# Joined attentions of a hybrid block: the full-array work of a group in three blocks instead of two

## The chip, the cores and the metric

One core of a Trainium2 chip runs the whole program in one launch. The metric is the time of the program on the device in microseconds (us). TensorE (PE in the profile) multiplies matrices, VectorE (DVE), ScalarE (ACT) and GpSimd (POOL) work on rows of 128 partitions, and PSUM is the memory of eight banks into which TensorE writes.

## The reference

Eight samples of 512 x 128 float32 pass through eight residual layers: attention A, a mixture of experts, attention B, the same mixture of experts, a linear attention, an adapter with experts, an attention with relative positions, and the adapter again. The change touches only attention A and attention B. Each of them is a causal attention with 16 heads of 8 channels:

```
q, k, v = (layernorm(x) @ Wq), (layernorm(x) @ Wk), (layernorm(x) @ Wv)     # 16 heads of 8
dot     = where(causal, q @ k.T * scale, -inf)                              # 512 x 512 for each head
x       = x + softmax(dot) @ v @ Wo
```

## The kernel before

The kernel handles two samples (a and b) in one turn of a loop and takes four turns. In each turn both samples go through the eight layers. `pe_attn(p, ...)` is TensorE's program for one attention layer of both samples at once ("joined"); it is called twice in a turn (p = 0 and 1), so it runs eight times in all.

**Groups and jobs.** The 32 heads (16 of a, then 16 of b) form 8 groups of 4. A group has 12 row jobs and 12 column jobs. A row job (L1049) computes scores with queries on the partitions, so that VectorE can take the row maximum (L1684, `row_max`); a column job (L1088) computes the same scores again, transposed and with the maximum already subtracted from q, so that ScalarE can take the exponential (L742) into `prob4`, and GpSimd then zeroes the diagonal blocks above the causal line (L531). Both kinds contract over 32 partitions only: each job occupies one of four 32-row strips of TensorE's array, and four jobs can run beside each other. A float32 matmul leaves two records in the profile. Row jobs 0 to 3 of a group have 512 columns, jobs 4 to 7 have 384, jobs 8 to 11 have 256 + 128. Column jobs 0 to 3 have 512 columns, 4 to 7 have 384, and 8 to 11 have 256 + 128 in two matmuls.

**The order on TensorE.** The order is written out by hand. Step k of the loop issues row job k and column job k - 16 (`LEAD` = 16). In the code `at` is the column job's number within its group g, so that k modulo 12 is `at` + 4 modulo 12. This text names a step by k modulo 12. Full-array work comes between steps:

- after step 2 the maxima are transposed (`max_columns`, L1059), the weighted heads of an earlier group are transposed back to rows (`head_rows`, L961), and a projection (L1028, "project") follows; `weigh_group(g, [0, 1])` (L1103), the first half of the product of probabilities and values, follows too. It has 16 records of 512 and 384 columns;
- after step 7 comes `weigh_group(g - 1, [2, 3])` (L1103, 16 records of 256 and 128 columns) and another projection.

Projections and a few single pieces of work stand in the table `BEHIND`, by k: at k = 67 the values of sample b are computed as well (L1035), and at k = 79 and 86 the output of sample a is transposed (L1121) and projected (L1129) in place of a projection.

**Buffers.** Row jobs and all full-array pieces but the weighing rotate over four PSUM banks; the order is the list `PLACES`, which is built from `BEHIND`. An entry waits until the entry four places earlier was read (`wait_place`). Column jobs rotate over three banks: job c waits for the exponential of job c - 3. From column job 81 on (`WIDE`, step k = 97) they have five banks. The weighing accumulates in bank 7; ScalarE copies it out after the group's second half (`group_columns`, L709), and `head_rows` waits for that copy. VectorE subtracts the maxima from q (`shift_q`, L1693) and divides the weighted heads by their sums (`heads_out`, L1655, L1656) after its row maximum 2 of each group. ScalarE moves projections out (L726 for q, L728 for k) at the step at which they stand in `BEHIND`.

**The tail.** Row jobs end with k = 95. After it the steps k = 96 to 111 issue column jobs alone, with the layer norm for the mixture of experts behind column job 90 (`HOOK`, L927), and then its router (L1209).

Of the kernel before, what the change touches and what calls it, by code (L numbers as in the profile page):

```python
# [66 lines left out]
ROWS4 = 3 * G4  # L67
GROUPS = 2 * NG
JOBS = ROWS4 * GROUPS
LEAD = 16  # L70
# [1 line left out]
HOOK = JOBS - 6  # L72


BEHIND = {26: [("norm", 0)], 31: [("project", 8)], 38: [("project", 9)], 43: [("project", 10)],
          50: [("project", 11)], 55: [("project", 12)], 62: [("project", 13)], 67: [("values", 0), ("project", 14)],
          74: [("project", 15)], 79: [("out_columns", 0)], 86: [("out", 0)]}
PLACES = []
for k in range(JOBS):
    PLACES.append(("row", k))  # L80
    if k % ROWS4 == 2 and k > ROWS4:
        PLACES.append(("max", k // ROWS4 - 1))
        if k // ROWS4 >= 3:
            PLACES.append(("heads", k // ROWS4 - 3))
    PLACES += BEHIND.get(k, [])
PLACE = {entry: at for at, entry in enumerate(PLACES)}
# [23 lines left out]
def build(nc, a_x, a_wq, a_wk, a_wv, a_wo, b_wattn, b_wout, m_ws, m_bs, m_wg, m_wu, m_wd,  # L110
# [9 lines left out]
    with ExitStack() as ctx:  # L120
# [53 lines left out]
        values = val_row[:, :, 0:H * BELOW].rearrange("p t (h d) -> p t h d", h=H)  # L174
# [22 lines left out]
        stage, at = part(0, [NSTAGE, P])  # L197
        stage_qk, at = part(at, [2, P])
        stage_gate, at = part(at, [P])
        rel_res, at = part(at, [2 * P])  # L200

        q_st, at = part(0, [H // 2, T], BF16)
        k_st, at = part(at, [H // 2, T], BF16)
        ring_at = at
        res, at = part(ring_at, [2, T])
        k_parts, at = part(at, [3, T], BF16)
        q_parts, at = part(ring_at + 3072, [3, T + 2], BF16)
# [12 lines left out]
        q_masked1, at = part(ring_at + 2 * T + 3 * T // 2, [2, IC, NT * H], BF16)  # L220
# [4 lines left out]
        r_neg_max, at = part(ring_at + RING * COLS, [RING, NT])  # L225
        sc, at = part(at, [H, len(BLOCKS), P])
        r_rden, at = part(at, [2, NT, G4])

        silu, at = part(at4, [2, T])
        hidden, at = part(at, [HSLOTS, T])  # L230
        lg, at = part(at, [NT, E])
        gt, at = part(at, [NT, E, E])
        eq, at = part(at, [NT, E, E])
        rank, at = part(at, [NT, E])
        top, at = part(at, [NT])
        lgd, at = part(at, [NT, E])
        ex, at = part(at, [NT, E])
        mixes, at = part(at, [2, NT, E])
        tot, at = part(at, [NT])

        l_qT, at = part(0, [NC2, T])
        l_kT, at = part(at, [NC2, T])
        l_k, at = part(at, [NT, H * DM])
        l_v, at = part(at, [NT, H * DM])
        l_vk, at = part(at, [NT, H * DM])
        l_wt, at = part(at, [2, 2, NT, P])
        l_st, at = part(at, [2, NT - 1, P])
        l_tmp, at = part(at, [2, NT, P])
        l_sq, at = part(at, [2, T])
        l_sqk, at = part(at, [2, 512])  # L250
        l_beta, at = part(at, [NT, H])
        l_ssum, at = part(at, [2, NT, H])
        l_rec, at = part(at, [2, NT, H])
        l_inv, at = part(at, [2, NT, H])

        pooled, at = part(0, [1])
        pool_rep, at = part(at, [P])
        d_hid, at = part(at, [KD, T])
        d_up, at = part(at, [KD, P])
        d_lg, at = part(at, [E])  # L260
        d_negm, at = part(at, [1])
        d_ex, at = part(at, [E])
        d_z, at = part(at, [1])
        d_gt, at = part(at, [E, E])
        d_eq, at = part(at, [E, E])
        d_rank, at = part(at, [E])
        d_w, at = part(at, [E])
        d_s, at = part(at, [1])
        d_w4, at = part(at, [KD])
        d_wT, at = part(at, [P])  # L270
# [3 lines left out]
        def bank(n):  # L274
            return psum[:, n, :]
# [217 lines left out]
        def column_head(c):  # L493

            return (c + 2) % G4

        def pad_bank(i):

            return (3, 7, 4, 5)[i % 4]
# [10 lines left out]
        def column_bank(c):  # L510

            return 3 + c % 3 if c < WIDE else 1 + (c - WIDE) % 5
# [208 lines left out]
        def act_attn(eng, p, scale):  # L721
            def stack(i, bk):
                eng.wait_ge(p_qk, 2 * GROUPS * p + i + 1)
                G = i // 2 % NG
                if i % 2 == 0:
                    m = eng.activation(q4[:, G, :], bank(bk), ACT.Copy, scale=scale)  # L726
                else:
                    m = eng.activation(k4[:, G, :], bank(bk), ACT.Identity, bias=k_one[:, 0:1])  # L728
                m.then_inc(p_st, 1)

            def out_columns(n, bk):
                eng.wait_ge(a_oT, n + 1)
                eng.activation(xnTs[n % 2][:, :], bank(bk), ACT.Copy).then_inc(a_oTs, 1)

            for i in range(2 * NG):
                stack(i, pad_bank(i))
            for c in range(JOBS):
                g, hh, j = c // ROWS4, column_head(c), c % ROWS4 // G4
                if g >= 2 and c % ROWS4 == 0:
                    eng.wait_ge(s_pv, GROUPS * p + g - 1)  # L740
                eng.wait_ge(s_col, JOBS * p + c + 1)
                eng.activation(prob4[:, g % 2, hh, C_AT[j]:C_AT[j] + C_N[j]], bank(column_bank(c))[:, 0:C_N[j]],  # L742
                               ACT.Exp).then_inc(s_exp, 1)
                if g >= 1 and c % ROWS4 == 5:
                    group_columns(eng, (g - 1) // NG, GROUPS * p + g - 1, 7, s_pv, GROUPS * p + g)
                for what, i in BEHIND.get(c + LEAD, []):
                    if what == "norm":
                        act_norm(eng, attn_call(2 * p + 1), row_bank((what, i)))
                    if what == "project":
                        stack(i, row_bank((what, i)))  # L750
                    if what == "out_columns":
                        out_columns(2 * p, row_bank((what, i)))
                if c == HOOK + 2:
                    act_norm(eng, moe_call(2 * p), 6)
            g = GROUPS - 1
            moe_exp(eng, 2 * p)
            group_columns(eng, 1, GROUPS * p + g, 7, s_pv, GROUPS * (p + 1))
            moe_silu(eng, 2 * p, 0)
            out_columns(2 * p + 1, 6)
# [231 lines left out]
        def pe_attn(eng, p, w):  # L991
# [101 lines left out]
            def weigh_group(g, keys):  # L1093

                last = min(keys[-1], 2)
                eng.wait_ge(s_keep, JOBS * p + ROWS4 * g + G4 * (last + 1))
                eng.wait_ge(a_v, 2 * p + g // NG + 1)
                if g >= 1:
                    eng.wait_ge(a_cols, GROUPS * p + g)
                for s in keys:  # L1100
                    for hh in range(G4):
                        h = G4 * (g % NG) + hh
                        m = eng.matmul(bank(7)[32 * hh:32 * hh + 32, P * s:T],  # L1103
                                       val_row[:, s, BELOW * h:BELOW * h + 32],
                                       prob4[:, g % 2, hh, C_COL[s]:C_COL[s] + T - P * s],
                                       start=(s == 0), stop=(s == NT - 1))
                if keys[-1] == NT - 1:
                    m.then_inc(s_pv, 1)
# [50 lines left out]
            for k in range(3 * NG, JOBS + LEAD):  # L1159
                if k < JOBS:  # L1160
                    score_rows(k)
                idle = (k + 2) % G4
                if 2 * NG + 2 <= k < LEAD - 2 and idle != 1:
                    eng.wait_ge(p_st, 2 * GROUPS * p + 5 + idle)
                    fill_strip(idle, pad_bank(idle))
                g, at = (k - LEAD) // ROWS4, (k - LEAD) % ROWS4
                if k >= LEAD:
                    score_columns(k - LEAD)
                    if k - LEAD == HOOK:
                        eng.wait_ge(s_shift, GROUPS * (p + 1))  # L1170
                        pe_norm(eng, moe_call(2 * p), 6)
                if k >= LEAD and g >= 1 and at == 3:
                    weigh_group(g - 1, [2, 3])
                if k % ROWS4 == 2 and k >= ROWS4:
                    if k < JOBS + 3:
                        max_columns(k // ROWS4 - 1)
                    if g >= 1:
                        head_rows(g - 1)
                for what, i in BEHIND.get(k, []):
                    behind(what, i)  # L1180
                if k >= LEAD and at == 10:
                    weigh_group(g, [0, 1])
            if p == 0:
                eng.wait_ge(experts_in, 16 * len(expert_loads))
# [396 lines left out]
        def _(eng):  # L1581
# [87 lines left out]
            def attn(p, loaded_x=None):  # L1669
# [29 lines left out]
                for k in range(JOBS + 3):  # L1699
# [9 lines left out]
                    if k % ROWS4 == 2 and k >= ROWS4:  # L1709
                        shift_q(k // ROWS4 - 1)  # L1710
                        if k // ROWS4 >= 3:
                            heads(k // ROWS4 - 3)
                    for entry in BEHIND.get(k, []):
                        if entry[0] == "values":
# [378 lines left out]
```

## Time and profile before

| | us |
|---|---|
| median of 3 runs | 3846.09 |
| lowest and highest run | 3843.22, 3848.20 |
| the profiled execution's own time | 3842.31 |
| its span, first to last instruction | 3840.4 |
| TensorE busy in the span | 3608.5 |
| VectorE, ScalarE, GpSimd busy | 2288.8, 1735.2, 824.6 |
| granted TensorE clock, mean | 0.994 |

The busy time of an engine is the sum over its instructions, and overlapping matmuls count once. In the timeline a row merges neighbouring instructions of one line: its first column is the start of the first, the second the time from there to the end of the last. Ends of matmuls are modelled, so starts are the better marks.

### The profile page before, as it was taken

Reading aid. Unit: us, or ns where it says so; the run is one execution under the profiler, and the core shown is the slowest. Engines: PE = TensorE matmul, PEld = TensorE weight load, DVE = VectorE, ACT = ScalarE, POOL = GpSimd, SP = SyncE. Lnnn points to the kernel's source line nnn. Section 1 sums busy time; section 2 is a strip of 40 time slices with the busy share of each in tenths; the row PEclk is TensorE's granted clock in tenths of the full one; section 3 lists DMA queues with packets and bytes.
Section 4 is the critical chain, followed back from the end, with each engine's and each line's share of the span. In section 5 each row is a group of like instructions: output and inputs, shape, how many; then the busy total and the mean of one; then the engine's idle time right before and its main releaser. Section 6 shows DMA issues by size and latency. Waiting matters only on the chain.

```text
span 3840.4 us, 78752 instructions
## 1 busy us (share of the span) xinstructions
PE 3608.5 (94%) x31071; PEld 2406.5 (63%) x31167; DVE 2288.8 (60%) x7514; ACT 1735.2 (45%) x3546; POOL 824.6 (21%) x1374
## 2 busy tenths in 40 slices
PE   6999999988999999998899999999889999999988
PEld 3656567666565667766556566776655656677665
DVE  4546455677654645577755554557675555455876
ACT  2425333466442523356644252335664335233656
POOL 3203023311210302332021030333302102033330
PEclk8999999999999999999999999999999999999999
DMA  3000000000000000000000000000000000000000
GB/s 88 1 1 2 1 1 1 2 1 2 13 1 1 2 1 1 1 2 2 1 13 1 1 2 1 1 1 2 2 7 8 1 1 1 1 1 1 2 2 9
DMA packets 27032, 17.47 MB, mean 5 GB/s; under 512 B 9425, under 2 KB 26274, under 8 KB 26658
## 3 DMA queue, kind: packets, MB, share of 16 engines
q1 hardware_dynamic: 26658, 12.32, 1.2%
q8 instruction: 254, 4.16, 0.5%
q14 instruction: 120, 0.98, 0.1%
HBM read 10.22 MB, written 2.10 MB: 3 GB/s over the span
## 4 chain that ended last, share of the span: by engine, by line
PE 71%; DVE 11%; POOL 7%; ACT 6%; issue 3%; SPq 1%; DVEq 0%; another core or an unknown queue 0%
PE banks L1237 9%; PE banks L1199 8%; PE banks L1204 8%; PE banks L1049 5%; PE banks L1088 5%; POOL work L564 5%; PE banks L1103 4%; PE banks L1028 3%; PE banks L1291 3%; PE banks L1499 3%; PE banks L1353 2%; ACT work L872 2%; ACT work L866 2%; PE banks L1512 2%; DVE work L1973 2%
## 5 line engine op out<-in xcount | busy, mean ns | idle before, releaser
L1684 DVE CUSTOM_DVE_ANT_0 work<-banks,mask_row 128x512 f32<-128x512 f32 (+3 forms) x1024 | 433.9, 486 | 279.3 <-PE banks L1049 279.2
L719 ACT ACTIVATE work<-banks 128x512 f32<-128x512 f32 x352 | 210.2, 597 | 672.2 <-PE banks L1199 657.0
L1775 DVE TENSOR_TENSOR work<-work,banks 128x512 f32<-128x512 f32 x352 | 242.1, 688 | 444.8 <-PE banks L1204 423.5
L520 POOL TENSOR_TENSOR rstd<-rstd,half 128x4 f32<-128x4 f32 x65 | 65.6, 1009 | 1948.2 <-DVE rstd L1608 1948.2
L742 ACT ACTIVATE work<-banks 128x384 f32<-128x384 f32 (+1 forms) x768 | 358.8, 534 | 252.2 <-PE banks L1088 251.6
L1237 PEld LDWEIGHTS banks<-wd,work 128*128 128x128 f32 (+2 forms) x4096 | 357.5, 189 | 179.9 <-issue 179.9
L1088 PE MATMUL banks<-work 32*128 32x512 f32 (+3 forms) x2048 | 443.7, 464 | 6.5 <-DVE work L1684 3.9
L1049 PE MATMUL banks<-work 32*128 32x384 f32 (+3 forms) x2048 | 405.2, 456 | 11.9 <-ACT work L728 6.4
L1237 PE MATMUL banks<-wd,work 128*128 128x128 f32 (+2 forms) x4096 | 376.6, 279 | 0.0
L531 POOL TENSOR_SCALAR_AFFINE_SELECT work<-work 128x128 f32<-128x128 f32 (+1 forms) x768 | 253.4, 333 | 458.8 <-ACT work L742 435.5
L1088 PEld LDWEIGHTS banks<-work 32*128 32x128 f32 x2048 | 243.0, 183 | 76.8 <-ACT work L742 39.4
L1049 PEld LDWEIGHTS banks<-work 32*128 32x128 f32 x2048 | 217.8, 184 | 114.8 <-issue 77.7
L866 ACT ACTIVATE work<-work 128x512 f32<-128x512 f32 (+3 forms) x512 | 244.6, 553 | 85.0 <-DVE work L1989 85.0
L1973 DVE TENSOR_TENSOR work<-work,banks 128x512 f32<-128x512 f32 (+1 forms) x384 | 211.7, 593 | 71.5 <-PE banks L1473 50.5
L1499 PE MATMUL banks<-ident,work 128*128 128x128 f32 x1280 | 194.5, 283 | 46.7 <-ACT work L872 46.7
L1983 DVE CUSTOM_DVE_ANT_0 work<-banks,mask_row 128x512 f32<-128x512 f32 (+3 forms) x512 | 224.0, 485 | 18.8 <-PE banks L1484 18.8
L872 ACT ACTIVATE work<-banks 128x512 f32<-128x512 f32 (+1 forms) x384 | 187.6, 523 | 80.4 <-PE banks L1499 75.6
L1450 PEld LDWEIGHTS banks<-work,relT 128*128 128x128 bf16 x6144 | 186.7, 98 | 24.8 <-DVE work L540 11.8
L1450 PE MATMUL banks<-work,relT 128*128 128x64 bf16 x6144 | 189.7, 193 | 9.5 <-DVE work L540 8.8
L1499 PEld LDWEIGHTS banks<-ident,work 128*128 128x128 f32 x1280 | 136.5, 141 | 95.6 <-ACT work L872 76.9
L564 POOL TENSOR_SCALAR_AFFINE_SELECT work<-work 128x256 f32<-128x256 f32 x256 | 179.0, 739 | 47.6 <-DVE work L1959 47.6
L1199 PE MATMUL banks<-xnT_a,wg 128*128 128x512 f32 x352 | 186.3, 611 | 0.0
(320 smaller groups left out, 6627.2 us busy)
## 6 DMA issues: line engine op xcount, KB each, us to landing
x_a<-in_L_attn_a_x_dram SPq DMA_DIRECT2D x5, 256.0 KB, 2.9
x_b<-in_L_attn_a_x_dram SPq DMA_DIRECT2D x4, 256.0 KB, 3.9
wg<-in_L_ffn_Wg_dram SPq DMA_DIRECT2D x2, 512.0 KB
wu<-in_L_ffn_Wu_dram SPq DMA_DIRECT2D x2, 512.0 KB
wd<-in_L_ffn_Wd_dram SPq DMA_DIRECT2D x16, 64.0 KB
out_dram<-x_a SPq DMA_DIRECT2D x4, 256.0 KB
out_dram<-x_b SPq DMA_DIRECT2D x4, 256.0 KB
wk_l<-in_L_attn_a_Wk_dram SPq DMA_DIRECT2D x1, 512.0 KB, 3.6
```

The source lines that it names most:

```text
L564: eng.affine_select(out=v, in_=v, compare_op=ALU.is_gt, fill=0.0, base=IC * c, pattern=[[0, H], [1, IC]], channel_multiplier=-1).then_inc( ...
L742: eng.activation(prob4[:, g % 2, hh, C_AT[j]:C_AT[j] + C_N[j]], bank(column_bank(c))[:, 0:C_N[j]], ACT.Exp).then_inc(s_exp, 1)
L866: eng.activation(v, v, ACT.Exp, bias=r_neg_max[:, h % RING, t:t + 1]).then_inc(r_p, 1)
L1049: m = eng.matmul(bank(row_bank(("row", k)))[:, col:col + N], q4[own, g % NG, P * t:P * t + P], k4[own, g % NG, 0:N], start=True, stop=True)
L1088: m = eng.matmul(bank(column_bank(c))[:, col:col + N], k4[own, g % NG, P * s:P * s + P], q4[own, g % NG, P * s:T], start=True, stop=True)
L1199: eng.matmul(bank(i % 2), wg[:, i, :], xnTs[n % 2][:, :], start=True, stop=True).then_inc(m_g, 1)
L1204: eng.matmul(bank(2 + i % 2), wu[:, i, :], xnTs[n % 2][:, :], start=True, stop=True).then_inc(m_u, 1)
L1237: m = eng.matmul(bank(expert_bank(e))[:, P * t:P * t + P], hidden[row:row + rows, i % HSLOTS, P * t:P * t + P], wd[row:row + rows, i, :], ...
L1450: m = eng.matmul(bank(k % 4)[:, 64 * (q % 8):64 * (q % 8) + 64], relT[:, rp, first:first + P], q_masked[c % 2][:, qp, q % IC, :], start=(g ...
L1499: m = eng.transpose(bank(5 + k % 2)[:, P * (b - first):P * (b - first) + P], r_prob[:, h % RING, ROW_AT[t] + P * s:ROW_AT[t] + P * s + P], ...
L1684: m = eng.tensor_tensor_reduce(out=summed[:, k % 2, col:col + N], in0=bank(bk)[:, col:col + N], in1=mask_row[:, T - N:T], scale=1.0, scala ...
L1973: eng.tensor_tensor(v, v, bank(r)[:, 0:JOB_N[j]], ALU.add).then_inc(r_sum, 1)
```

## The change

Three things move. `weigh_group(g - 1, [0, 1])` leaves its place after step 2 (behind the transposes and the projection) and gets one of its own after step 5; for the last group alone it stays where it was. `weigh_group(g - 1, [2, 3])` and the `BEHIND` entries beside it move from after step 7 to after step 9 (k = 31 becomes 33, and so on). ScalarE's `group_columns` moves from after exponential 5 to after exponential 7 of a group. `PLACES`, and with it the rotation of banks, follows from the new `BEHIND`.

```diff
-BEHIND = {26: [("norm", 0)], 31: [("project", 8)], 38: [("project", 9)], 43: [("project", 10)],
-          50: [("project", 11)], 55: [("project", 12)], 62: [("project", 13)], 67: [("values", 0), ("project", 14)],
-          74: [("project", 15)], 79: [("out_columns", 0)], 86: [("out", 0)]}
+BEHIND = {26: [("norm", 0)], 33: [("project", 8)], 38: [("project", 9)], 45: [("project", 10)],
+          50: [("project", 11)], 57: [("project", 12)], 62: [("project", 13)], 69: [("values", 0), ("project", 14)],
+          74: [("project", 15)], 81: [("out_columns", 0)], 86: [("out", 0)]}
@@ act_attn
-                if g >= 1 and c % ROWS4 == 5:
+                if g >= 1 and c % ROWS4 == 7:
                     group_columns(eng, (g - 1) // NG, GROUPS * p + g - 1, 7, s_pv, GROUPS * p + g)
@@ pe_attn
-                if k >= LEAD and g >= 1 and at == 3:
+                if k >= LEAD and g >= 1 and at == 1:
+                    weigh_group(g - 1, [0, 1])
+                if k >= LEAD and g >= 1 and at == 5:
                     weigh_group(g - 1, [2, 3])
...
-                if k >= LEAD and at == 10:
+                if k >= LEAD and at == 10 and g == GROUPS - 1:
                     weigh_group(g, [0, 1])
```

## Rows read from the trace of the kernel before

**Rows 1.** The page's first part: busy time of each engine and share of the span.

```profile
PE 3608.5 (94%) x31071; PEld 2406.5 (63%) x31167; DVE 2288.8 (60%) x7514; ACT 1735.2 (45%) x3546; POOL 824.6 (21%) x1374
```

**Rows 2.** Windows, one group each: start:end, length, busy of PE, PEld, DVE, ACT, POOL.

```profile
83.28:95.77 12.49, 12.49 (x125) 7.69 (x121) 7.81 (x35) 7.22 (x15) 3.96 (x12) 1.00 0.01 1
95.77:108.31 12.54, 12.54 (x124) 7.68 (x120) 7.81 (x35) 7.34 (x15) 3.96 (x12) 1.00 0.01 2
108.31:122.03 13.72, 13.72 (x133) 8.59 (x129) 8.51 (x36) 7.22 (x15) 3.96 (x12) 1.00 0.00 1
```

**Rows 3.** Timeline of TensorE, one group: start, length, line, operation and tile.

```profile
95.77 0.69 PE L1049 MATMUL banks<-work 32*128 32x512 f32 x1
...
97.16 1.06 PE L1088 MATMUL banks<-work 32*128 32x512 f32 x2
...
98.61 0.59 PE L1088 MATMUL banks<-work 32*128 32x512 f32 x1
99.12 0.86 PE L1103 MATMUL banks<-work,values 128*32 128x256 f32 x16
99.80 1.04 PE L1028 MATMUL banks<-xnT_b,spaced_q_a 128*32 128x512 f32 x8
100.77 0.48 PE L1049 MATMUL banks<-work 32*128 32x256 f32 x1
...
104.79 0.66 PE L1059 MATMUL banks<-ident,work 128*128 128x128 f32 x4
105.28 0.60 PE L961 MATMUL banks<-ident,xnT_a 128*128 128x128 f32 x4
105.81 1.06 PE L1028 MATMUL banks<-xnT_b,padded_k_a 128*32 128x512 f32 x8
106.70 1.69 PE L1103 MATMUL banks<-work,values 128*32 128x512 f32 x16
108.31 0.69 PE L1049 MATMUL banks<-work 32*128 32x512 f32 x1
...
111.61 0.86 PE L1103 MATMUL banks<-work,values 128*32 128x256 f32 x16
```

**Rows 4.** Timeline of ScalarE, same group; in brackets its idle time before and the releaser.

```profile
96.98 1.53 ACT L742 ACTIVATE work<-banks 128x384 f32<-128x384 f32 x3 [1.90 <-PE banks L1088]
98.69 1.14 ACT L742 ACTIVATE work<-banks 128x512 f32<-128x512 f32 x2 [0.17 <-PE banks L1088]
...
101.77 0.87 ACT L742 ACTIVATE work<-banks 128x384 f32<-128x384 f32 x2 [0.26 <-PE banks L1088]
102.52 0.60 ACT L709 ACTIVATE xnT_a<-banks 128x512 f32<-128x512 f32 x1
103.00 1.28 ACT L742 ACTIVATE work<-banks 128x384 f32<-128x384 f32 x3
...
106.95 0.69 ACT L728 ACTIVATE work<-banks,k_one 128x512 f32<-128x512 f32 x1 [1.56 <-PE banks L1028]
```

**Rows 5.** Timeline of VectorE, same group.

```profile
96.92 0.69 DVE L1684 CUSTOM_DVE_ANT_0 work<-banks,mask_row 128x512 f32<-128x512 f32 x1 [2.51 <-PE banks L1049]
...
101.72 0.42 DVE L1684 CUSTOM_DVE_ANT_0 work<-banks,mask_row 128x256 f32<-128x256 f32 x1 [2.19 <-PE banks L1049]
...
105.78 0.68 DVE L1693 TENSOR_TENSOR work<-work,banks 128x512 f32<-128x512 f32 x1
...
106.67 0.29 DVE L1656 TENSOR_TENSOR xn_a<-banks,work 128x128 f32<-128x128 f32 x1
```

**Rows 6.** Timeline of TensorE and ScalarE in the tail of an attention.

```profile
149.44 1.34 PE L1088 MATMUL banks<-work 32*128 32x384 f32 x14
150.72 0.66 PE L961 MATMUL banks<-ident,xnT_b 128*128 128x128 f32 x4
151.50 1.71 PE L1103 MATMUL banks<-work,values 128*32 128x512 f32 x16
...
149.71 0.60 ACT L709 ACTIVATE xnT_b<-banks 128x512 f32<-128x512 f32 x1
150.19 1.28 ACT L742 ACTIVATE work<-banks 128x384 f32<-128x384 f32 x3
```

## Prediction, made before the changed kernel ran

> **What bounds the kernel now.** I read the busy line of the page first: TensorE is busy 94% of the span and every other engine 60% or less [rows 1]. A busy TensorE is not a full one here, because four jobs of 32 rows overlap and a stretch counts as busy while only one of them runs. So I went to the timeline of one attention and cut it where TensorE changes between strips and full-array work. The pattern repeats: a plain group takes 12.49 to 12.54 us, one with extra work 13.72, all at a granted clock of 1.00 [rows 2]. In a plain group, counted from its first step (step 3) [rows 3]:
>
> - strips, steps 3 to 7: 95.77 to 99.12, 3.35 us, and 108.31 to 111.61, 3.30 us, in the next group. The groups of 12.49 us have 3.30, which I use.
> - short block, weighing [2, 3] and projection: 0.68 + 0.97 = 1.65 us.
> - strips, steps 8 to 2: 100.77 to 104.79, 4.02 us.
> - long block: transposes 0.49 + 0.53, projection 0.89, weighing [0, 1] 1.61 us, together 3.52.
>
> Sum 3.30 + 1.65 + 4.02 + 3.52 = 12.49 us.
>
> What sets the length of the strips is not TensorE's streaming but ScalarE, through the three column banks. After a block the first exponential starts 1.21 us later (96.98 against 95.77), or 1.00 us (101.77 against 100.77) [rows 3, 4]. In the first stretch column job 3 needs the bank of job 0. The three exponentials from 96.98 take 1.53 us and are jobs 11, 0 and 1; the two of 512 columns from 98.69 take 1.14, so one takes about 0.63 and they follow each other every 0.5. Exponential 0 therefore ends at about 98.0, job 3 starts then, and the block follows at 99.12, 1.12 us later. In the second stretch column job 10 needs exponential 7: 1.00 us, two exponentials 0.75, the copy of the group's columns 0.48 (102.52 to 103.00), then exponentials 6 and 7, of which the second ends at 103.87 (1.28 for three, less 0.41), and 0.92 later the block starts at 104.79. VectorE waits too: 2.51 us in the long block and 2.19 us in the short one [rows 5]. Both readers of PSUM are thus idle about 5 of 12.5 us, since their banks run empty in a block and refill more than a microsecond after it.
>
> **The change part by part.** No arithmetic is added or removed. I count one plain group of the new order in the same way.
>
> *Stretch X, steps 3 to 5.* Three row and three column jobs. Their banks are free: column jobs 11, 0 and 1 need exponentials 8, 9 and 10, done in the block before. So only streaming counts. The old trace shows these very jobs: the last pass of column job 1 starts at 97.16, 1.39 us after the start, and a block follows a last pass of 512 columns by 0.51 us (98.61 to 99.12) [rows 3]. X = 1.90 us. Two waits could hold it. Row job 5 needs `heads_out`: VectorE ended it at 106.96, 2.17 us after the old long block began [rows 5]; the new block is 1.99 us and VectorE enters it 0.1 us later than before (its row maxima 10, 11, 0, 1, 2 need 2.95 us from 0.95, to 3.90, against a stretch of 2.79), so this is ready 0.3 us after the start of X, where row job 5 has its strip free only near 0.98. The copy of the projection, L728, came 0.25 us after that projection ended and lasted 0.69 [rows 4]. It had the weighing as cover; now it ends 0.94 us into X and the first exponential comes at 1.21, so it costs nothing, with 0.27 us to spare.
>
> *Block of weighing [0, 1].* 1.61 us in the trace behind another full-array piece, up to 1.65 with 0.04 for the entry from strips, which the weighing [2, 3] shows (0.68 us for 384 columns at the rate of 896 in 1.5). I take 1.64. The diagonals that it needs were zeroed long before.
>
> *Stretch Y, steps 6 to 9.* Column job 5 needs exponential 2. The first reader of a 512-column job starts 1.15 us after the start (VectorE, 96.92 against 95.77) [rows 3, 5], exponential 2 takes 0.62, and job 5 with 384 columns should take 0.85 to the block (below: less than the 0.92 of job 10, which has the same columns in two matmuls; above: the 1.12 of a 512-column job). Y = 1.15 + 0.62 + 0.85 = 2.62 us. Ends: 1.00 + 0.62 + 0.75 = 2.37 and 1.21 + 0.62 + 1.12 = 2.95.
>
> *Short block*: unchanged, 1.65 us.
>
> *Stretch Z, steps 10 to 2.* Column job 10 needs exponential 7. Exponentials 6 and 7 end 1.00 + 0.87 = 1.87 us after the start, and 0.92 later the block starts: Z = 2.79 us. The copy of the group's columns is now behind exponential 7 and no longer in this chain; it ends near 2.4 us, before `head_rows` needs it at 2.79 + 0.49. Ends 2.6 and 3.0, from the 0.2 us by which restarts differ.
>
> *Block of transposes and projection*: 0.49 + 0.53 + 0.97 = 1.99 us; the projection is now followed by strips, which costs 0.97 where 0.89 was measured in front of full-array work [rows 3].
>
> Sum: 1.90 + 1.64 + 2.62 + 1.65 + 2.79 + 1.99 = 12.59 us against 12.49, so 0.10 us more in a group. What the 0.48 us copy and the shorter waits give back is eaten by the third restart. An attention has six such groups between the transposes at k = 26 and k = 98: 0.6 us.
>
> The Trainium skill ("TensorEngine Tiling (Array Packing)", Key Properties) says that changing the tiling mode drains TensorE, which speaks against a third block. By this rule each of the 56 added pairs of changes costs a drain. The trace agrees that a block waits for the strips, but prices the change itself at 0.04 us on entry and 0.08 us on leaving [rows 3], 7 us over the run, and these are already in the terms above; without them the sum would be no change in a group.
>
> *The tail.* Here all columns have five banks. `head_rows` of group 6 ran at 150.72, after the copy L709 that stood at 149.71 in front of three exponentials [rows 6]. After the change this copy stands behind exponential 91, the second of those three. Column job 91 comes behind the layer-norm transposes and starts near 149.5, its exponential at 150.5 to 150.9, the copy to 151.5. `head_rows` then starts at 151.5, ends at 152.03, and the last weighing [0, 1] starts there and not at 151.50. Before, that weighing waited only for the zeroed diagonal of job 91. So the tail is 0.5 us longer (0 if the steps before it run earlier, 0.9 if the weighing block at k = 101 is late too).
>
> Per attention 0.6 + 0.5 = 1.1 us, and eight attentions make 9 us. The profiled execution took 3842.31 us, span 3840.4 and 1.9 around it; the changed one would take 3851. The median of the runs shown is 3.8 us higher, so on its scale 3855.
>
> **The rivals.**
>
> *The readers are fed evenly (faster).* VectorE's wait of 2.51 us in the long block stands for it: with 1.5 us less of full-array work in one piece, one long wait shrinks. If Y and Z run at their lower ends and X is unchanged, a group takes 12.59 - 0.25 - 0.2 = 12.14 us, 0.35 less than before, times 48 groups = 17 us, of which the tail takes 4 back: 3833. Against it: the third block brings a new wait of the same kind, since X offers only three jobs of each kind, about 1.5 us of reading that begins 1.2 us after the start of X and is over before the 1.64 us block ends. The Trainium skill (same page, PSUM Bottleneck) holds that after a fourfold tiling the copies out of PSUM may become the limit. Were they alone the limit, a group would be VectorE's 7.81 us; the rows show 12.49, so this is only a direction.
>
> *Everything cancels (no change).* The 0.10 us per group is a difference of terms read to 0.05 to 0.1. If Y ends where its 384-column job suggests (0.75) the group is even, and the tail alone gives 4 us: 3850.
>
> *The third restart is paid in full (slower still).* The place is stretch Y: if job 5 takes the 1.12 us of a 512-column job and the restart 1.21, and row job 5 waits for `heads_out` in X, which decides as soon as VectorE ends it more than 1 us after the start of X, a group has 0.33 to 0.45 more than my sum. 48 x 0.4 = 19 us on top: 3874.
>
> *The moved bank rotation stalls strips.* Entries four places apart are now row jobs everywhere but behind the transposes, so no new slow releaser stands in front of a step. I give it nothing of its own.
>
> **How the numbers follow.** A measurement of this kernel tells about 0.2%, 7.7 us, from no change, so slower begins at 3853.8 and faster below 3838.4. My forecast (3848 to 3862) has 0.5, no change or nearly 0.27, the faster rival 0.12, the slower rival 0.11. Of my forecast's 0.5 about 0.38 lies above 3853.8. That gives slower 0.50, the same 0.38, faster 0.12. The range 3840 to 3868 leaves about 0.1 on either side.
>
> **What would show it.** In the new timeline: block starts 1.9, 6.2 and 10.6 us after the start of a group, a period of 12.55 to 12.65 us; stretches of 1.90, 2.6 and 2.8 us; ScalarE idle for well over a microsecond three times a group and not twice; L709 no longer between exponentials 5 and 6; `head_rows` of the tail directly behind L709. The prediction is wrong if a period is below 12.4 us (then Y or Z are shorter than their chains through the exponentials), or if the layers outside the two attentions change.

## The result, and the profile after

The changed kernel took 3854.80 us (median of 11 runs, 3852.11 to 3857.34) against 3846.09 us (11 runs, 3841.77 to 3851.93): ratio 1.0022, 95% interval 1.0012 to 1.0031, so 8.7 us slower. Run again beside other runs of before it took 3857.1 against 3843.99, ratio 1.0035 (1.0022 to 1.0049). The forecast was 3855. The profiled execution took 3857.3 us, 15.0 more than the profiled one of before.

The first part of the page after answers to [rows 1]. No engine's share moved by more than a point.

```profile
PE 3622.4 (94%) x31167; PEld 2379.8 (62%) x31167; DVE 2293.7 (59%) x7514; ACT 1738.8 (45%) x3546; POOL 822.5 (21%) x1374
```

Two plain groups, the columns as in [rows 2]. Both have 12.63 us, where before it was 12.49 and 12.54.

```profile
81.51:94.14 12.63, 12.63 (x125) 7.11 (x121) 7.90 (x35) 7.23 (x15) 3.94 (x12) 1.00 0.01 1
94.14:106.77 12.63, 12.63 (x125) 7.11 (x121) 7.90 (x35) 7.28 (x15) 3.94 (x12) 1.00 0.01 2
```

The timeline of TensorE in the second of them answers to [rows 3]. Take the starts of the blocks: 96.05, 100.34, 104.75.

```profile
94.14 0.69 PE L1049 MATMUL banks<-work 32*128 32x512 f32 x1
...
95.53 0.59 PE L1088 MATMUL banks<-work 32*128 32x512 f32 x1
96.05 1.71 PE L1103 MATMUL banks<-work,values 128*32 128x512 f32 x16
97.69 0.58 PE L1049 MATMUL banks<-work 32*128 32x384 f32 x1
...
99.50 0.91 PE L1088 MATMUL banks<-work 32*128 32x384 f32 x2
100.34 0.86 PE L1103 MATMUL banks<-work,values 128*32 128x256 f32 x16
101.01 1.04 PE L1028 MATMUL banks<-xnT_b,spaced_q_a 128*32 128x512 f32 x8
101.98 0.48 PE L1049 MATMUL banks<-work 32*128 32x256 f32 x1
...
104.75 0.66 PE L1059 MATMUL banks<-ident,work 128*128 128x128 f32 x4
105.24 0.60 PE L961 MATMUL banks<-ident,xnT_a 128*128 128x128 f32 x4
105.77 1.07 PE L1028 MATMUL banks<-xnT_b,padded_k_a 128*32 128x512 f32 x8
106.77 0.69 PE L1049 MATMUL banks<-work 32*128 32x512 f32 x1
```

ScalarE in the same group, against [rows 4]. L709 now stands between exponentials 7 and 8 (the row of two is 6 and 7).

```profile
95.36 1.53 ACT L742 ACTIVATE work<-banks 128x384 f32<-128x384 f32 x3 [0.39 <-PE banks L1088]
98.85 2.09 ACT L742 ACTIVATE work<-banks 128x512 f32<-128x512 f32 x4 [1.97 <-PE banks L1088]
102.12 0.60 ACT L726 ACTIVATE work<-banks 128x512 f32<-128x512 f32 x1 [1.18 <-PE banks L1028]
102.98 0.87 ACT L742 ACTIVATE work<-banks 128x384 f32<-128x384 f32 x2 [0.26 <-PE banks L1088]
103.74 0.60 ACT L709 ACTIVATE xnT_a<-banks 128x512 f32<-128x512 f32 x1
```

VectorE, against [rows 5]. It now waits three times, 0.86 + 1.68 + 2.15 = 4.69 us, where it waited twice, 2.51 + 2.19 = 4.70. The change spread its idle time and took none away.

```profile
95.30 0.69 DVE L1686 CUSTOM_DVE_ANT_0 work<-banks,mask_row 128x512 f32<-128x512 f32 x1 [0.86 <-PE banks L1049]
...
98.63 0.56 DVE L1686 CUSTOM_DVE_ANT_0 work<-banks,mask_row 128x384 f32<-128x384 f32 x1 [1.68 <-PE banks L1049]
...
102.94 0.42 DVE L1686 CUSTOM_DVE_ANT_0 work<-banks,mask_row 128x256 f32<-128x256 f32 x1 [2.15 <-PE banks L1049]
```

The tail of the second attention, against [rows 6]: `head_rows` (L961) waits 1.12 us for the copy L709, which stands behind exponential 91.

```profile
388.64 0.95 PE L1088 MATMUL banks<-work 32*128 32x384 f32 x14
390.71 0.63 PE L961 MATMUL banks<-ident,xnT_b 128*128 128x128 f32 x4 [1.12 <-ACT xnT_b L709]
391.26 1.71 PE L1103 MATMUL banks<-work,values 128*32 128x512 f32 x16
...
389.58 0.49 ACT L742 ACTIVATE work<-banks 128x384 f32<-128x384 f32 x1 [0.82 <-PE banks L1088]
389.97 0.59 ACT L709 ACTIVATE xnT_b<-banks 128x512 f32<-128x512 f32 x1
```

From its first projection to the router's first matmul an undisturbed attention takes 110.5 us before and 112.4 us after: 1.89 us more, of which 0.79 lies in the six groups and 1.09 in the tail. Times eight that is 15 us.

### The profile page after: what moved, and what is told of

Its sections match the earlier page's. It is cut to its first block, busy times and chain, and to the rows that moved or that the text cites. A ratio compares the mean times of both kernels' runs of the same rounds, so it can differ in the third digit from the quotient of the medians.

```text
span 3855.4 us, 78848 instructions
## 1 busy us (share of the span) xinstructions
PE 3622.4 (94%) x31167; PEld 2379.8 (62%) x31167; DVE 2293.7 (59%) x7514; ACT 1738.8 (45%) x3546; POOL 822.5 (21%) x1374
## 4 chain that ended last, share of the span: by engine, by line
PE 73%; DVE 11%; POOL 7%; ACT 6%; issue 3%; SPq 1%; DVEq 0%; another core or an unknown queue 0%
PE banks L1239 9%; PE banks L1201 8%; PE banks L1206 8%; PE banks L1049 6%; PE banks L1088 6%; POOL work L564 5%; PE banks L1103 4%; PE banks L1028 3%; PE banks L1293 3%; PE banks L1501 3%; PE banks L1355 2%; ACT work L872 2%; ACT work L866 2%; PE banks L1514 2%; DVE work L1975 2%
## 5 line engine op out<-in xcount | busy, mean ns | idle before, releaser
L1088 PE MATMUL banks<-work 32*128 32x384 f32 (+3 forms) x2048 | 451.2, 462 | 7.7 <-DVE work L1686 5.1
L1049 PE MATMUL banks<-work 32*128 32x384 f32 (+3 forms) x2048 | 391.3, 459 | 11.9 <-ACT work L728 6.4
L1049 PEld LDWEIGHTS banks<-work 32*128 32x128 f32 x2048 | 204.7, 184 | 165.9 <-issue 101.8
L1088 PEld LDWEIGHTS banks<-work 32*128 32x128 f32 x2048 | 228.3, 183 | 53.7 <-ACT work L742 19.4
```

Of the source, the lines that this page charges most:

```text
L1049: m = eng.matmul(bank(row_bank(("row", k)))[:, col:col + N], q4[own, g % NG, P * t:P * t + P], k4[own, g % NG, 0:N], start=True, stop=True)
L1088: m = eng.matmul(bank(column_bank(c))[:, col:col + N], k4[own, g % NG, P * s:P * s + P], q4[own, g % NG, P * s:T], start=True, stop=True)
```

## The experiments

All medians stand against runs of the kernel before on the same chip. "Attention" is an undisturbed one as above; before has 110.5 us, 12.49 in a plain group and 11.43 in the tail (from the last max transposes to the router).

| kernel | strips of steps | plain group | tail | attention | median us | ratio and interval |
|---|---|---|---|---|---|---|
| before | 5, 7 | 12.49 | 11.43 | 110.5 | | |
| changed | 3, 4, 5 | 12.63 | 12.52 | 112.4 | 3854.80 | 1.0022 (1.0012 to 1.0031) |
| changed, copy behind 5 | 3, 4, 5 | 12.63 | 11.74 | 111.6 | 3849.48 | 1.0012 (1.0003 to 1.0021) |
| changed, tail as before | 3, 4, 5 | 12.63 | 11.43 | 111.3 | 3845.03 | 1.0002 (0.9993 to 1.0011) |
| third block only | 3, 2, 7 | 12.31 | 11.95 | 109.7 | 3837.05 | 0.9982 (0.9973 to 0.9991) |
| short block and copy moved | 7, 5 | 12.34 | 12.81 | 111.1 | 3846.92 | 1.0004 (0.9995 to 1.0013) |
| before, copy behind 3 | 5, 7 | 12.34 | 11.29 | 109.6 | 3835.38 | 0.9979 (0.9970 to 0.9988) |
| before, copy behind 7 | 5, 7 | 12.34 | 12.00 | 110.3 | 3846.72 | 1.0007 (0.9997 to 1.0016) |
| third block behind step 6 | 4, 1, 7 | 13.20 | 11.95 | 115.0 | 3878.89 | 1.0094 (1.0079 to 1.0110) |
| new version | 3, 2, 7 | 12.16 | 11.29 | 108.3 | 3828.04 | 0.9964 (0.9951 to 0.9978) |
| new version, block behind 8 | 3, 3, 6 | 12.29 | 11.29 | 109.2 | 3827.76 | 0.9958 (0.9943 to 0.9973) |

**The copy in the tail.**

```diff
 # changed kernel
-                if g >= 1 and c % ROWS4 == 7:
+                if g >= 1 and c % ROWS4 == 5:
                     group_columns(...)
```

> The changed kernel with ScalarE's copy of the weighed columns (L709) behind exponential 5 again and not 7. Theory (the tail's head_rows waits for this copy): plain groups stay at 12.63 us, since the copy moves from behind the chain of exponentials 6 and 7 into the short block, where ScalarE is idle; in the tail the 1.12 us wait of head_rows goes and the stretch from the last max transposes to the router falls from 12.5 to about 11.8 us: 0.7 us x 8 = 5.5 us faster than the changed kernel. Rival (the last weighing waits for the diagonal of job 91 anyway): under 0.3 us in an attention, under 2 us in all.

Groups stayed at 12.63 and the tail fell from 12.52 to 11.74, 0.78 us, as expected. The late copy is worth 0.8 us in an attention, and in plain groups it does not matter in the changed order. The distance of the medians from before fell from 8.7 to 4.8 us, by 3.9, where 5.5 was expected.

**The tail alone.**

```diff
 # changed kernel; group 7 keeps the places and the copy of before
+                if k >= LEAD and 1 <= g < GROUPS - 1 and at == 1:
                     weigh_group(g - 1, [0, 1])
+                if k >= LEAD and g >= 1 and at == (3 if g == GROUPS - 1 else 5):
                     weigh_group(g - 1, [2, 3])
+                if k >= LEAD and at == 10 and g >= GROUPS - 2:
                     weigh_group(g, [0, 1])
```

> The changed kernel, but the last group's blocks and copy stand as in the kernel before (weighing [0, 1] of group 6 behind step 98, its [2, 3] behind step 103, copy behind exponential 5). Theory: plain groups stay at 12.63 us and the stretch from the last max transposes to the router is the 11.43 us of before: 1.08 us x 8 = 8.6 us faster than the changed kernel, and 0.8 us x 8 = 6.3 us slower than before. Rival (the tail only looks longer, its work is taken from the group before it): the tail's gain is given back in the group before k = 98 and the total moves by under 3 us.

The tail is exactly that of before, 11.43 us, and the groups kept 12.63. The distance of the medians from before fell from 8.7 to 0.3 us, by 8.4, where 8.6 was expected. By the ratio it is 0.8 us (-2.7 to 4.2) above before where the trace has 6.3: here the trace and the medians do not agree (below).

**The third block by itself.**

```diff
 # kernel before
+                if k >= LEAD and g >= 1 and at == 1:
+                    weigh_group(g - 1, [0, 1])
                 if k >= LEAD and g >= 1 and at == 3:
                     weigh_group(g - 1, [2, 3])
...
-                if k >= LEAD and at == 10:
+                if k >= LEAD and at == 10 and g == GROUPS - 1:
```

> The kernel before with one part of the change: weighing [0, 1] gets its own place after step 5; the short block stays after step 7 and the copy behind exponential 5. Theory (a stretch costs what its chain of exponentials costs, and three steps after a block are free of it because three column banks are empty): strips 1.90 + 1.05 + 4.02 us, blocks 1.64 + 1.65 + 2.02, together 12.3 us in a plain group against 12.49, so 0.2 x 6 less in an attention, less 0.4 given back in the tail: 0 to 8 us faster than before. Rival (each added block pays drain and restart in full): 12.6 us or more in a group, as with the whole change, 5 to 13 us slower.

Faster than before, 12.31 us in a group. TensorE's timeline of one such group:

```profile
93.91 0.69 PE L1049 MATMUL banks<-work 32*128 32x512 f32 x1
...
95.82 1.71 PE L1103 MATMUL banks<-work,values 128*32 128x512 f32 x16
97.46 0.58 PE L1049 MATMUL banks<-work 32*128 32x384 f32 x1
...
98.53 0.86 PE L1103 MATMUL banks<-work,values 128*32 128x256 f32 x16
99.20 1.04 PE L1028 MATMUL banks<-xnT_b,spaced_q_a 128*32 128x512 f32 x8
100.17 0.48 PE L1049 MATMUL banks<-work 32*128 32x256 f32 x1
...
104.19 0.66 PE L1059 MATMUL banks<-ident,work 128*128 128x128 f32 x4
```

Strips 1.91 + 1.07 + 4.02 = 7.00 us, as expected, against 3.30 + 4.02 = 7.32 before. The five steps 3 to 7 take 2.98 us in two pieces and 3.30 in one. The third block adds 0.14 us to the blocks (5.31 us for 5.17), so as such it is a gain of 0.18 us, and the rival is out.

**The short block and the copy moved, without the third block.**

```diff
 # kernel before, with the BEHIND of the change and the copy behind 7
-                if k >= LEAD and g >= 1 and at == 3:
+                if k >= LEAD and g >= 1 and at == 5:
                     weigh_group(g - 1, [2, 3])
```

> The kernel before with the other part: the short block and its BEHIND entries after step 9, the copy behind exponential 7; weighing [0, 1] stays in the long block, so there are two blocks. Theory: strips 4.05 (job 5 waits for exponential 2) + 2.79 us, blocks 1.65 + 3.55, together 12.0 us in a plain group: the copy's 0.48 us is out of the chain. 0.45 us x 6 less in an attention, 0.5 to 0.6 given back in the tail by the late copy: 15 to 20 us faster than before. Then the third block alone costs 0.6 us in a group of the changed kernel. Rival (the place of the short block costs, not the third block): 12.5 us or more and no gain.

A miss. The group fell to 12.34 us and not to 12.0, and the tail rose to 12.81, more than the late copy explains (0.57 to 0.78 us of the 1.38), so the whole did not gain: the median is 2.2 us above before, where 15 to 20 us less was expected. Nor is the 0.15 us in a group due to the block's new place: the copy moved by itself gives the same 12.34 us (below). The first stretch took 4.41 us where I had 4.05:

```profile
96.95 0.69 PE L1049 MATMUL banks<-work 32*128 32x512 f32 x1
...
101.36 0.86 PE L1103 MATMUL banks<-work,values 128*32 128x256 f32 x16
...
98.17 1.53 ACT L742 ACTIVATE work<-banks 128x384 f32<-128x384 f32 x3 [1.90 <-PE banks L1088]
99.87 2.08 ACT L742 ACTIVATE work<-banks 128x512 f32<-128x512 f32 x4 [0.18 <-PE banks L1088]
```

The chain goes round twice here: exponential 11 frees the bank for column job 2, whose exponential starts only at 99.87, and column job 5 waits for that one. I had let exponential 2 follow exponential 1 at once.

**The copy in the kernel before.** One line, `c % ROWS4 == 5` to 3, and in a second kernel to 7.

> The kernel before with one line changed: ScalarE's copy of the weighed columns stands behind exponential 3 and not 5, so that it runs while the short block's projection does. Theory (the copy's 0.48 us stands in the chain of exponentials 4 to 7 for which column job 10 waits): the stretch of steps 8 to 2 falls from 4.02 to about 3.6 us (VectorE's row maxima allow 3.6), a plain group from 12.49 to about 12.1, the tail is unchanged: 0.4 x 7 x 8 = 20 to 24 us faster than before. Rival (VectorE or streaming sets this stretch): 4.0 us and no gain.

> The kernel before with the copy behind exponential 7, as in the change, and nothing else. Theory: plain groups as with the copy behind exponential 3, about 12.1 us; in the tail head_rows waits for the late copy, 0.6 to 0.8 us in an attention. 15 to 18 us faster than before. Rival (the late copy holds something in plain groups too): groups above 12.3 us.

Both are misses in size. The groups fell to 12.34 us in both, 0.15 and not 0.4. In the medians the copy behind 3 gained 9.0 us where 20 to 24 were expected, and the copy behind 7 gained nothing (2.3 us above before, within the interval) where 15 to 18 were. With the copy gone the stretch of steps 8 to 2 takes 3.87 us (102.51 to 106.38):

```profile
102.51 0.48 PE L1049 MATMUL banks<-work 32*128 32x256 f32 x1
...
105.81 0.59 PE L1049 MATMUL banks<-work 32*128 32x512 f32 x1
105.85 0.59 PE L1088 MATMUL banks<-work 32*128 32x256 f32 x3
106.38 0.66 PE L1059 MATMUL banks<-ident,work 128*128 128x128 f32 x4
...
104.58 0.42 DVE L1684 CUSTOM_DVE_ANT_0 work<-banks,mask_row 128x256 f32<-128x256 f32 x1
104.92 0.29 DVE L1684 CUSTOM_DVE_ANT_0 work<-banks,mask_row 128x128 f32<-128x128 f32 x1
```

Row job 2 waits for row maximum 10, the third after the block, which VectorE ends at 105.2. Its last pass starts at 105.81, and 0.57 us later the block. So the row banks, through VectorE, stood 0.15 us behind the column banks. In the tail the copy behind 7 costs 0.57 us more than behind 5 (12.00 against 11.43), and behind 3 it saves 0.14.

**The step from three to four.** As the third block alone, but behind step 6 (`at == 2`).

> As b_third (weighing [0, 1] in a place of its own, short block behind step 7), but the weighing behind step 6 and not step 5: stretches of 4, 1 and 7 steps instead of 3, 2 and 7. Theory (a stretch of three steps finds its three column banks empty; the fourth column job waits for the first exponential after the block): the first stretch takes about 1.21 + 0.5 + 1.0 = 2.7 us against 1.91, the second 0.85 to 0.95 against 1.07; a plain group 12.9 to 13.0 us against 12.31; 30 us slower than b_third. Rival (a stretch costs by its streaming, the waits at its end are hidden by the block): under 12.4 us, as b_third.

```profile
94.92 0.69 PE L1049 MATMUL banks<-work 32*128 32x512 f32 x1
...
97.73 1.71 PE L1103 MATMUL banks<-work,values 128*32 128x512 f32 x16
99.37 0.58 PE L1049 MATMUL banks<-work 32*128 32x384 f32 x1
...
100.43 0.86 PE L1103 MATMUL banks<-work,values 128*32 128x256 f32 x16
...
96.14 1.53 ACT L742 ACTIVATE work<-banks 128x384 f32<-128x384 f32 x3 [0.39 <-PE banks L1088]
...
96.68 0.29 PEld L1088 LDWEIGHTS banks<-work 32*128 32x128 f32 x2 [0.58 <-ACT work L742]
```

The first stretch grew from 1.91 to 2.81 us for one step more, and the second, one step shorter, stayed at 1.06: 0.89 us in a group and 42 us in the run against the third block behind step 5. This is the sharpest of the tests. The fourth column job waits for the first exponential after the block: its weights are loaded at 96.68, after 0.58 us of waiting for ScalarE, whose first exponential starts at 96.14. A stretch of one step costs as much as one of two. The effect was larger than expected: the group has 13.20 us and not 12.9 to 13.0, and the run is 42 us slower and not 30.

**New versions.** The third block behind step 5, the short block behind step 7 as before, the copy behind exponential 3, the last group in the old order; then the same with the short block behind step 8.

```diff
 # third block only
-                if g >= 1 and c % ROWS4 == 5:
+                if g >= 1 and c % ROWS4 == 3:
...
+                if k >= LEAD and 1 <= g < GROUPS - 1 and at == 1:
                     weigh_group(g - 1, [0, 1])
...
+                if k >= LEAD and at == 10 and g >= GROUPS - 2:
                     weigh_group(g, [0, 1])
```

> A version after the theory: weighing [0, 1] behind step 5, short block behind step 7 as before, copy behind exponential 3, the last group in the old order. Stretches 1.91 + 1.07 + 3.6 us, blocks 5.31 us: 11.9 us in a plain group, tail 11.4 us. 0.6 x 6 + 0.4 in an attention: 28 to 34 us faster than before. Rival (once the copy is out of the chain VectorE is late and the third block costs): 12.1 us or more, no better than b_copy3.

> As t_best, but the short block and its BEHIND entries stand behind step 8 and the copy behind exponential 4: stretches of 3, 3 and 6 steps. Theory (three column jobs behind a block wait for no exponential): stretches 1.91, 1.75 (streaming of three steps) and 3.3 us (row job 2 waits for row maximum 10, the second after the block), blocks 5.31: 12.2 to 12.3 us in a plain group, within 5 us of t_best in all. Rival (every further step behind a short stretch costs as in t_step6, 0.9 us): 12.9 us or more in a group, 35 us slower than t_best.

The first took 3828.04 us, 16.3 less than before, where 28 to 34 were expected. Its group has 12.16 us and not 11.9, again because of the 3.87 us stretch. That is the group of the rival (12.1 us or more), but the run is not the rival's: it gained 7 us more than the copy behind 3 did alone. In the second the strips are 1.91, 1.81 and 3.25 us: the middle stretch starts at 96.23 and the last at 99.69, and their blocks at 98.04 and 102.94.

```profile
94.59 1.71 PE L1103 MATMUL banks<-work,values 128*32 128x512 f32 x16
96.23 0.58 PE L1049 MATMUL banks<-work 32*128 32x384 f32 x1
...
98.04 0.86 PE L1103 MATMUL banks<-work,values 128*32 128x256 f32 x16
98.71 1.04 PE L1028 MATMUL banks<-xnT_b,spaced_q_a 128*32 128x512 f32 x8
99.69 0.48 PE L1049 MATMUL banks<-work 32*128 32x256 f32 x1
...
102.94 0.66 PE L1059 MATMUL banks<-ident,work 128*128 128x128 f32 x4
```

Three steps behind a block cost their streaming alone, at two places. The medians of the two versions do not differ (3828.04 and 3827.76), though by its attentions the first should be 6.7 us ahead (108.3 against 109.2 us, times eight). Both are faster than both kernels of this case.

**The two kernels again.**

> The changed kernel unaltered. An undisturbed attention of its trace is 1.87 us longer than one of before, 15.0 us in eight, while the medians differ by 8.7. Theory (the attentions' times are fixed by the order of work; single executions differ by stalls of about 1.6 us whose number varies): again 112.4 us in an undisturbed attention, and the medians differ by 9 to 15 us. Rival (the attention itself varies between executions): another period than 12.63 us.

> The kernel before unaltered, profiled a second time. Theory: 110.5 us in an undisturbed attention again, and more stalls of about 1.6 us than in the first profile, which was among the fast executions (3842.31 against a median of 3846.09). Rival: periods other than 12.49 us.

The periods and the undisturbed attentions came out the same to 0.03 us, and the medians of the changed kernel and of before differ by 13.1 us, within the 9 to 15 expected. Before, run again, took 3846.18 against 3843.99 (1.0003, 0.9993 to 1.0012).

## Why the prediction was right

By its own steps, for a plain group, in us:

| | predicted | measured |
|---|---|---|
| X, steps 3 to 5 | 1.90 | 1.91 |
| weighing [0, 1] | 1.64 | 1.64 |
| Y, steps 6 to 9 | 2.62 | 2.65 |
| short block | 1.65 | 1.64 |
| Z, steps 10 to 2 | 2.79 | 2.77 |
| transposes and projection | 1.99 | 2.02 |
| sum | 12.59 | 12.63 |

Both waits that could have held X stayed hidden. VectorE ended `heads_out` at 94.43, 0.29 us after the start of X (predicted 0.3), and the first exponential came at 95.36, 1.22 after it (1.21). The price of a restart, read from a block of the old order, carried over to a block at another place. For Y the 0.85 us from the freeing exponential to the block was an estimate between rows, and the whole stretch is off by 0.03.

**The tail was mis-sized.** I said 0.5 us; it is 1.09. The experiments split it. The late copy is 0.78 of it (12.52 to 11.74), where I had 0.5. The other 0.31 is what remains with the copy in its old place. It goes with the last group's blocks, since with them back in the old order the tail is 11.43 again. There are now three stretches of columns in place of two ahead of the layer norm; why they cost just this much was not taken apart. I had named that as an upper end (0.9 "if the weighing block at k = 101 is late too") and left it out of the sum. With 0.79 in the groups for my 0.6, an attention is 1.89 us longer and not 1.1.

**So part of the agreement of 3855 with 3854.8 is luck.** By the trace the eight attentions add 15 us, not 9; the medians show 8.7 in one set and 13.1 in the other. Single executions differ by several microseconds. Within an attention the traces show what the expectations call stalls of about 1.6 us: for a few microseconds, at places that change from one execution to the next, TensorE's granted clock falls. The first profile of before has this in one tail, which takes 13.03 us and not 11.43; its second profile has it in two. There TensorE was busy 3.52 of the 4.00 us from 1325 to 1329, at a granted clock of 1.00. From 1329.30 to 1332.60 it was granted 0.50 (the third number from the end of the first row), the lower of its two levels (1.2 GHz of 2.4), and the weighing [0, 1] took 2.69 us where it has 1.71.

```profile
1329.30:1332.60 3.30, 3.30 (x20) 1.63 (x22) 2.48 (x15) 0.66 (x2) 0.79 (x2) 0.50 0.00 0
...
1330.67 2.69 PE L1103 MATMUL banks<-work,values 128*32 128x512 f32 x16
```

The clock goes with the gap between traces and medians too. The changed kernel's median is 6.3 us better against before than its attentions say (8.7 against 15), and its 11 runs had a mean granted clock of 0.9963, the highest of all. The runs of before beside the experiments had 0.9936 to 0.9942 (those beside the changed kernel's first set have no clock on record). With the tail as before (0.9955) the median is 5.9 us better than its attentions say, with the copy behind 5 (0.9948) 3.9, with short block and copy moved (0.9949) 2.6. In the second set of the changed kernel (0.9938) it is 1.9, and with only the copy moved behind 7, which had the lowest clock (0.9919), the median is 3.7 us worse. The match is not exact: at 0.9950 stand both the block behind 8 (5.3 us better) and the third block behind step 6 (1.3). So the clock is a part of the gap and is not shown to be all of it, and why one set of runs was granted more than another stays open.

**The cause that I gave for the sum was half right.** I wrote that the third restart eats what the copy gives back. The third block alone makes the group 0.18 us shorter; the short block and the copy moved make it 0.15 shorter, as the copy does alone; all together make it 0.14 longer. The loss lies in where the steps went: from the third block alone to the whole change, steps 8 and 9 move from the last stretch into the middle one. The last falls from 4.02 to 2.77, 1.25 less (0.15 of it is due to the copy), and the middle rises from 1.07 to 2.65, 1.58 more, since with four steps it falls into the chain of restart, exponential 2 and column job 5. The two steps leave a stretch in which readers are already running and enter one in which TensorE must wait for them. And the copy gave back only 0.15 of its 0.48 us in the old order, with VectorE's chain next behind it.

The Trainium skill's rule that changing the tiling mode drains TensorE ("TensorEngine Tiling (Array Packing)", Key Properties) would have any third block cost something. The traces agree that a block waits for the strips, 0.51 us after the last pass of 512 columns starts, and that a third block adds 0.14 us to the blocks. But the third block alone is a net gain, so the number of changes is not what decides. The other rule weighed, on copies out of PSUM as the limit (same page, PSUM Bottleneck), fits in direction only: VectorE is busy 7.90 of 12.16 us in the new version.

Of the rivals, evenly fed readers did not come about: VectorE waits as long in all as before. The signs that I named were seen, but one of them was weak: ScalarE had three waits of over a microsecond before as well (1.90, 1.56 and 1.08), and VectorE's waits are the better mark.

## What to carry to other kernels

Where an engine alternates between filling a few buffers and other work, count the jobs of each stretch against the buffers. Here, with three banks, three jobs behind a block cost only their streaming, and the fourth waited for the first reader to start again (0.89 us in a group for that one step). The number of banks itself was not varied. So cut the stretches by the number of buffers and not to equal length, and let the one long stretch be long. A reader's side task, such as a copy, belongs where that reader is idle, behind the piece of work that produces its input; and an order tuned for the steady state should be checked in the tail, where this change cost 1.09 us in an attention and in its six groups together 0.79.

## What the runs showed of the hardware

At a granted clock of 1.00 the order of work fixes an attention to 0.03 us (110.51 to 110.54 us before, 112.39 to 112.41 changed); only the first attention of an execution is about 2 us longer (112.29 and 114.11 us). A tail in which the clock was 0.50 for 3.3 us took 1.6 us longer. A stretch of one step (a row job of 384 and a column job of 512 columns) and one of two steps cost the same, 1.06 and 1.07 us. The jobs lie in different strips, and in the stretch of two steps all four start within 0.02 us of each other (97.46 to 97.48, third block alone). I had expected 0.85 to 0.95 for the single one.
